# A graph attention and expert kernel: the first graph's index with evenly cut list transfers, its column cast first, and node positions found and scattered by groups of seven tiles

## The reference

```python
edge_index = jnp.stack([src, dst])                                  # 100,000 edges, 6250 nodes
x = x + gnn(_layernorm(x), edge_index, W, a_l, a_r)                 # 4 heads of 64 features
x = x + ffn(_layernorm(x)[None], W_gat, att_src, att_dst, ..., L0_ffn_edge_index)[0]   # 131,072 edges

# gnn: for each edge (row, col)
e   = leaky_relu(h_l[row] + h_r[col], 0.2)
m   = segment_max(e, row);  ex = exp(e - m[row])
att = ex / segment_sum(ex, row)[row]
out = segment_sum(att[:, :, None] * h[col], row)
```

## Time and profile before

| what | value |
|---|---|
| median of 3 runs | 3050.68 us (3048.28 to 3055.36) |
| profiled execution | 3046.62 us, span 3044.9 us |
| POOL busy | 1871.1 us (61%) |
| DVE busy | 1847.1 us (61%) |
| PE busy | 1694.7 us (56%) |
| ACT busy | 587.0 us (19%) |

### The profile page before, as it was taken

One profiled execution on the slowest core, in us unless ns is written; L12 is line 12 of the kernel. 1 busy time (PEld: TensorE's weight loads), 2 busy tenths in 40 slices (PEclk: granted clock), 3 DMA queues, 4 the chain that ended last, 5 costly groups with the idle time before them and its releaser, 6 DMA issues. The chain is left out here.

```text
span 3044.9 us, 25674 instructions
## 1 busy us (share of the span) xinstructions
PE 1694.7 (56%) x7316; PEld 1279.9 (42%) x7316; DVE 1847.1 (61%) x3710; ACT 587.0 (19%) x1135; POOL 1871.1 (61%) x1908
## 2 busy tenths in 40 slices
PE   4511430255655552666645268889797979786300
PEld 3411110234434341444335246667676767674200
DVE  7778783879977885766656224443434334347558
ACT  4300000123322220222224111212121211110000
POOL 0000457767777777777507677777777777777470
PEclk9755765677777775878775589899999999998655
DMA  5300302557666565666455322222222222227244
GB/s 160 51 0 0 95 6 77 170 192 242 222 221 200 192 224 156 211 218 228 166 207 153 78 70 43 43 53 43 55 40 46 43 43 43 43 55 212 74 127 157
DMA packets 203488, 354.57 MB, mean 116 GB/s; under 512 B 56043, under 2 KB 161442, under 8 KB 193842
## 3 DMA queue, kind: packets, MB, share of 16 engines
q0 software_dynamic: 73264, 122.14, 17.7%
q1 hardware_dynamic: 80889, 181.57, 17.0%
q10 hardware_dynamic: 49260, 50.05, 5.0%
HBM read 181.47 MB, written 171.59 MB: 116 GB/s over the span
## 5 line engine op out<-in xcount | busy, mean ns | idle before, releaser
L567 POOL DMA_INDIRECT at_ring<-table,e_col x872 | 831.9, 954 | 265.7 <-issue 265.7
L1800 POOL DMA_INDIRECT at_ring<-table,at_idx x792 | 784.4, 990 | 253.2 <-issue 233.4
L1892 PE MATMUL at_psS<-at_ring,at_hot 128*128 128x260 f32 x1584 | 436.7, 439 | 147.8 <-DVEq L1997 140.5
L1892 PEld LDWEIGHTS at_psS<-at_ring,at_hot 128*128 128x128 f32 x1584 | 319.5, 218 | 257.5 <-issue 84.3
L1368 PE MATMUL ffn_psY<-late_space 128*128 128x256 f32 x1568 | 356.9, 389 | 99.0 <-DVE late_space L1420 99.0
L1357 PE MATMUL ffn_psH<-xnT,late_space 128*128 x896 | 359.4, 561 | 69.0 <-ACT late_space L1392 60.8
L1420 DVE TENSOR_TENSOR late_space<-ffn_psY,ffn_b 128x256 f32<-128x256 f32 x196 | 82.5, 424 | 517.4 <-PE ffn_psY L1368 517.2
L1368 PEld LDWEIGHTS ffn_psY<-late_space 128*128 128x128 f32 x1568 | 305.8, 196 | 149.1 <-DVE late_space L1420 101.8
L1914 ACT ACTIVATE at_ring<-at_psS 128x520 f32<-128x520 f32 (+1 forms) x432 | 237.7, 567 | 507.7 <-PE at_psS L1892 507.7
L1357 PEld LDWEIGHTS ffn_psH<-xnT,late_space 128*128 128x128 f32 x896 | 275.4, 310 | 143.2 <-ACT late_space L1392 65.0
L1992 DVE TENSOR_TENSOR at_ring<-at_ring,at_psW 128x1024 f32<-128x1024 f32 (+1 forms) x216 | 231.5, 1127 | 27.8 <-ACT at_ring L1905 19.6
(11 more groups left out here) (367 smaller groups left out, 2169.1 us busy)
## 6 DMA issues: line engine op xcount, KB each, us to landing
at_sums<-at_ring SPq DMA_DIRECT2D x72, 1452.0 KB, 6.0
products<-late_space ACTq DMA_DIRECT2D x28, 896.0 KB
late_space<-products SPq DMA_DIRECT2D x16, 896.0 KB, 11.8
at_ring<-table,e_col POOLq DMA_INDIRECT x872
at_ring<-table,at_idx POOLq DMA_INDIRECT x792, 3.3
at_sums<-at_ring SPq DMA_DIRECT2D x16, 768.0 KB, 3.3
late_space<-products ACTq DMA_DIRECT2D x12, 896.0 KB, 11.9
table<-np_rows SPq DMA_DIRECT2D x7, 910.0 KB, 4.2
```

Source lines behind the costliest of these rows:

```text
L567: g.indirect_dma_start(self.ring[z][:, k, 0:TW], None, self.table, bass.IndirectOffsetOnAxis(ap=self.runs.col[:, u * U + k:u * U + k + 1], ...
L1800: g.indirect_dma_start(self.ring[z][:, k, 0:self.TW], None, self.table, bass.IndirectOffsetOnAxis(ap=self.idx[:, z, k:k + 1], axis=0)).the ...
L1892: last = pe.matmul(self.psS[at % 2][:, k - lo, 0:TW], self.hot[:, b, k, :], rows[:, b * self.SUB + k, 0:TW], start=True, stop=True)
```

## The change

- The list of `prior` is loaded in two transfers (112 and 15 rows), `by_chain` in two (96 and 3), and so is the second graph's shifted list in `Runs.load_prior` (112 and 15).
- DVE casts the columns to `x.col` before it waits for `even` and `prior`.
- The first graph's positions are found by groups of seven tiles, between the tiles' counts. Their PE results lie in another PSUM tile (`att.psE`), since `turned` is still in use then. POOL makes its three `row0` gathers first and waits per group of seven scatters.
- In round 0, `weigh_rows` stands ahead of `short_levels`.
- For the second graph, `positions` is the same work in three calls, with two instructions in another order.

```diff
+EVENLY = (0, 112), (112, 127)
@@ Ranks
+    def count_past(self, pe):
         for i in range(t.T):
             last = pe.matmul(self.ps_many[:, i:i + 1], t.past[:, i, :], t.one[:, :], start=True, stop=True)
         last.then_inc(self.s_many, 1)
+    def nexts(self, pe, part, lo, hi):
+        pe.wait_ge(self.s_first, part + 1)
+        pe.matmul(self.ps_next[:, lo:hi], t.shift[:, :], t.first[:, lo:hi], start=True, stop=False)
+        pe.matmul(self.ps_next[:, lo:hi], t.corner[:, :], t.first[:, lo + 1:hi + 1], start=False, stop=True)\
+            .then_inc(self.s_next, 1)
+    def bases(self, v):
+        v.wait_ge(self.s_many, 1)
+        q.step(v.tensor_scalar(t.before_t[:, :], self.ps_many, 1.0, float(self.J), ALU.subtract, ALU.mult))
+    def firsts(self, v, lo, hi):
+        v.wait_ge(self.s_used, 2 * hi + 2)
...
+        v.sem_inc(self.s_first, 1)
+    def positions(self, v, part, lo, hi, start_idx):
+        v.wait_ge(self.s_next, part + 1)
...
@@ Runs.load_prior
-        a.dma_start(self.prior[1:P, :].bitcast(F32), self.code[0:P - 1, :]).then_inc(self.s_prior, 16)
+        for lo, hi in EVENLY:
+            a.dma_start(self.prior[lo + 1:hi + 1, :].bitcast(F32), self.code[lo:hi, :]).then_inc(self.s_prior, 16)
@@ ChainRuns.load
-        sp.dma_start(self.prior[1:P, :], codes[0:P - 1, :]).then_inc(self.s_even, 16)
-        sp.dma_start(self.by_chain, self.flat[0:x.slots].rearrange("(p m) -> p m", p=CHAINS)).then_inc(self.s_chain, 16)
+        for lo, hi in EVENLY:
+            sp.dma_start(self.prior[lo + 1:hi + 1, :], codes[lo:hi, :]).then_inc(self.s_even, 16)
+        chains = self.flat[0:x.slots].rearrange("(p m) -> p m", p=CHAINS)
+        for lo, hi in (0, 96), (96, CHAINS):
+            sp.dma_start(self.by_chain[lo:hi, :], chains[lo:hi, :]).then_inc(self.s_chain, 16)
@@ ChainRuns.set_starts
+        for b in range(x.T // BATCH):
+            g.wait_ge(self.s_starts, b + 1)
+            for t in range(b * BATCH, (b + 1) * BATCH):
...
@@ ChainRuns.vector
         for t in range(x.T):
             ranks.below(v, 0, 0, t)
-        ranks.positions(v, x.start_idx[:, :])
-        v.sem_inc(self.s_starts, 1)
+            b, k = divmod(t, BATCH)
+            if t == BATCH:
+                ranks.bases(v)
+            if b and k == 0:
+                ranks.firsts(v, found, t + 1)
+                found = t + 1
+            elif b and k == 2:
+                starts(b - 1)
+        ranks.firsts(v, found, x.T)
+        starts(batches - 1)
@@ ChainRuns.tensor
             ranks.rows(pe, 0, 0, t)
-        ranks.end_rows(pe)
+            b, k = divmod(t, BATCH)
+            if t == 0:
+                ranks.count_past(pe)
+            elif b and k == 1:
+                ranks.nexts(pe, b - 1, (b - 1) * BATCH, b * BATCH)
+        ranks.nexts(pe, batches - 1, (batches - 1) * BATCH, self.index.T)
@@ block two, DVE, round 0
                         att.scores(v, n0, z)
+                        att.weigh_rows(v, n0, z)
                         order2.short_levels(v, levels)
-                        att.weigh_rows(v, n0, z)
```

More of the change, by code:

```diff
@@ L384, in below @@
                             accum_out=t.n[:, bass.ds(at + i, 1), half]).then_inc(self.s_used, 1)
[L386 to L389, removed]
+    def count_past(self, pe):
+        t = self.t
+        for i in range(t.T):
             last = pe.matmul(self.ps_many[:, i:i + 1], t.past[:, i, :], t.one[:, :], start=True, stop=True)
         last.then_inc(self.s_many, 1)
[L392 to L394 removed]
@@ L396, in positions @@
-    def positions(self, v, start_idx):
-        t, T, q = self.t, self.t.T, self.q
-        q.eng = v
[L401 to L406, removed]
-        v.wait_ge(self.s_many, 1)
-        do(v.tensor_scalar(t.before_t[:, :], self.ps_many, 1.0, float(self.J), ALU.subtract, ALU.mult))
-        do(v.tensor_tensor(t.many[:, :], t.many[:, :], t.before_t[:, :], ALU.add))
-        do(v.tensor_scalar(t.first[:, 0:T], t.many[:, :], 0.0, None, ALU.max))
-        v.sem_inc(self.s_first, 1)
[L412 to L417, removed]
+    def nexts(self, pe, part, lo, hi):
+        t = self.t
+        pe.wait_ge(self.s_first, part + 1)
+        pe.matmul(self.ps_next[:, lo:hi], t.shift[:, :], t.first[:, lo:hi], start=True, stop=False)
+        pe.matmul(self.ps_next[:, lo:hi], t.corner[:, :], t.first[:, lo + 1:hi + 1], start=False, stop=True)\
+            .then_inc(self.s_next, 1)
@@ new lines, in positions @@
+    def positions(self, v, part, lo, hi, start_idx):
+        t, q, at = self.t, self.q, slice(lo, hi)
+        q.eng = v
+        v.wait_ge(self.s_next, part + 1)
+        q.step(v.tensor_tensor(t.count[:, at], self.ps_next[:, at], t.first[:, at], ALU.subtract))
+        q.step(v.tensor_scalar(t.last[:, at], self.ps_next[:, at], 1.0, 0.0, ALU.subtract, ALU.max))
+        q.wait()
+        q.step(v.tensor_scalar(t.none[:, at], t.count[:, at], 0.0, float(NOWHERE), ALU.is_equal, ALU.mult))
+        q.wait()
+        q.step(v.tensor_tensor(t.spare_t[:, at], t.first[:, at], t.none[:, at], ALU.add))
+        q.wait()
+        q.step(v.tensor_copy(start_idx[:, at], t.spare_t[:, at]))
+        q.wait()
@@ L469, in positions @@
         x, t, q = self.index, self.ranks.t, self.q
-        self.ranks.positions(v, x.start_idx[:, :])
+        self.ranks.bases(v)
+        self.ranks.firsts(v, 0, t.T)
+        self.ranks.positions(v, 0, 0, t.T, x.start_idx)
         q.step(v.tensor_tensor(t.last[:, :], t.last[:, :], t.none[:, :], ALU.add))
@@ L1610, in set_starts @@
         x = self.index
[L1611 to L1615, removed]
         for n in range(GROUPS):
@@ L1619, in set_starts @@
                                  bounds_check=x.T * P - 1, oob_is_err=False).then_inc(self.s_row0, 16)
+        for b in range(x.T // BATCH):
+            g.wait_ge(self.s_starts, b + 1)
+            for t in range(b * BATCH, (b + 1) * BATCH):
+                g.indirect_dma_start(self.starts, bass.IndirectOffsetOnAxis(ap=x.start_idx[:, t:t + 1], axis=0),
+                                     self.own[:, t, :], None, bounds_check=x.slots - 1, oob_is_err=False)\
+                    .then_inc(self.s_set, 16)
     def vector(self, v):
@@ L1653, in vector, with starts @@
         v.sem_inc(self.s_col, 1)
+        v.wait_ge(self.s_even, 48)
+        v.wait_ge(self.att.s_iota, 1)
+        ranks.past(v, self.even)
         ranks.differences(v, self.even, self.prior, self.itmp, self.itmp2)
+        def starts(b):
+            ranks.positions(v, b, b * BATCH, (b + 1) * BATCH, x.start_idx)
+            v.sem_inc(self.s_starts, 1)
+        batches, found = x.T // BATCH, 0
         for t in range(x.T):
             ranks.below(v, 0, 0, t)
-        ranks.positions(v, x.start_idx[:, :])
-        v.sem_inc(self.s_starts, 1)
+            b, k = divmod(t, BATCH)
[8 more added lines that the diff above has]
+        starts(batches - 1)
         rowf, new = self.rowf, self.colf
```

31 lines of the change are left out of this document (23 added, 8 removed).

## The result

The changed kernel takes 2979.2 us (median of 4 runs, 2975.94 to 2986.15); the kernel before, with one more run, 3051.73. The ratio is 0.9763, 95% interval 0.9751 to 0.9776: 2.4% faster, 72.5 us. The profiled execution took 2975.94 us, span 2974.2, which is 70.7 us under the span before. Block two starts 0.9 us earlier than before and block three 70.2 us earlier (DVE's first instruction there is at 1501.93 for 1572.10), so that 69.2 us of it arise in block two.

A forecast was written before the change was run, and what follows sets the result against it. Block two was bound first by hand-overs, then POOL until about unit 14, then DVE. Savings of 40.3 + 7.2 + 26 = 73.5 us from 3046.62 gave 2973.1 profiled, median 2977; range 2962 to 3006, own bounds 2968 to 2994.

The forecast's parts named there:

- Lists and cast: Block two's start: list lands before 321.9, POOL gets its index 15.2 us earlier, DVE's first count comes 7.8 us earlier.
- Groups on DVE: First graph's positions: seven sets at 1.6 us, 11.2 in all; positions end at 412.9, 2.2 us later than before.
- groups at full price: Rival: each group's PE trip stands open (4.6 us), index 20.5 us later; 53 us off, 2998; chance 0.10.
- Scatters: POOL, block two: scatters start after row0 gathers at 371.0, keep 73.9 us without starving, done at 444.9 for 485.25.
- the slower rival: Rival: scatters beside DVE's counts take 5.12 us each, POOL ends at 622; 104 us slower, 3155; chance 0.03.
- The wait that ends last: Before the seeds' load: SP waits for DVE's index at 448.3 instead of the scatters; 2.5 us of 40 lost.
- Unit 2: POOL in block two: waits for the stored seeds until 501.7, so this unit starts 40.3 us earlier.
- Slots: Round 0: POOL's waits of 1.58 and 5.64 us for slots go, 7.2 us gained, between 0 and 7.2.
- Second list: Second graph's shifted list, late in block two: landing 10.8 us after issue, DVE's wait some 3, 26 us gained.
- signs of being wrong: POOL waiting between groups, scatters over 2 us, second-list wait over 10 us, or DVE waiting for gathers in the last rounds.
- The second list did come sooner: Rival denied here: busy DMA engines bring the second graph's list no sooner in effect; 47.5 us off, 3003; chance 0.11.
- the cut into even pieces matters: Rival denied here: pieces bring neither list sooner, DVE starts 6.7 us later than forecast; 40.8 off, 3010; chance 0.04.

The follow-up runs named there:

- a5: The changed kernel with the shifted lists' two pieces of 113 and 14 rows instead of 112 and 15: 3004.4 us, ratio 0.9854 to the kernel before.
- a2: The changed kernel with all 49 tiles' positions found at once after the counts, no groups; repeated on another chip: 3008.8 us, ratio 0.9861 to the kernel before.
- a4: The changed kernel with groups of seven kept, but POOL scattering only after the last group; repeated on another chip: 3019.9 us, ratio 0.9903 to the kernel before.
- b3: The kernel before with only the groups of seven, scatters group by group and the row0 gathers first: 3023.7 us, ratio 0.9919.
- a3: The changed kernel with short_levels ahead of weigh_rows in round 0 again; repeated on another chip: 2984.2 us, ratio 0.9786 to the kernel before.
- b1: The kernel before with only the second graph's shifted list in pieces of 112 and 15 rows: 3022.0 us, ratio 0.9907.
- c1: The changed kernel with three groups (14, 21, 14 tiles) for seven and the row0 gathers last: 2979.8 us, ratio 0.9766 to the kernel before.

## Why the prediction was right

It said 2977 us, 73.5 us off; 2979.2 and 72.5 were measured. The mechanism of block two's first 200 us was right; the 26 us of the second list came out right by luck. Point by point:

- *Lists and cast.* This was right. Both lists land early, DVE begins `past` at 322.3, the first count comes at 335.13 (forecast 335.9), and POOL's index copy at 322.3 (323.4). a5 shows the cause.
- *Groups on DVE.* The positions were forecast 2.2 us later than before; they came 1.1 later, or 2.0 counted from the block's start. DVE's wait behind the small matmuls is 1.33 us, where 2 were forecast. PE's trips are covered except the last (0.76 us). The rival of groups at full price is out: six further sets and the matmuls together cost 9.0 us (a2 against a4), and at 4.6 us a set they would have cost 28.
- *Scatters.* Their end was forecast at 444.9 and measured at 441.3. They start at 369.27, not at 371. They keep 0.98 us beside the counts and slow down, to 4.11 at most, only beside DVE's wide instructions, as before, and POOL shows no more than its usual 0.30 us between groups. The starved scatters of the slower rival would have needed 3.0 us each, pause included, only to lose what the rest gained. With the rule of the Trainium skill, "SBUF — State Buffer", section "SBUF: two separate sides", by which DVE's two-port instructions keep GpSimd from writing descriptors, the trace agrees as far as the counts go: beside them a scatter takes its usual 0.98 us.
- *The wait that ends last.* This was right: the index took the place of the scatters, and the seeds start at 447.22 (forecast 448.3). a2 and b3 show the other order, where the scatters end last.
- *Unit 2.* Its start was forecast at 501.7 and measured at 501.50. Counted from the block's start it is 0.7 later than forecast.
- *Slots.* 7.2 us were forecast, and 6.2 measured at unit 6; a3 gives 6.3 us of waits back. It also held that DVE's three new waits for exponentials (2.06 us each) cost nothing.
- *POOL after that.* The forecast carried POOL's lead to the end unchanged; 2.2 us were lost over units 6 to 23. The page has the 792 gathers at 788.3 us of busy time for 784.4. Which of DVE's instructions slow them was not tried.
- *Second list.* The term was 26 us and 26.3 arrived, but by two errors that cancel, and that is luck. The step "landing 10.8 us like the store, a wait of 3" failed: the list landed in 4 to 5 us and no wait was left, so that 28.8 us were to be had. And the step "35.1 - 3.2 = 31.9 us before it meets POOL again" failed as well: it set the distance at unit 23 against the shortest distance at unit 9. DVE is nearest to POOL at unit 21. There it starts at 1442.98, 31.8 us behind the end of the gather (POOL's next copy, 1411.18), and the shortest distance in these rounds is 5.5 us (b1). That leaves 26.3 us of room, just what came. One of the signs of being wrong that the prediction names did appear: in the changed kernel DVE waits 6.26 us at unit 21 (1372.56), for 4.42 before, so POOL did take the bound back there.
- *Rivals.* The second list did come sooner (b1), and the cut into even pieces matters (a5).
- *The range.* The forecast's own bounds, added up again from the numbers beside them, give 2971 to 2994 and not 2968 to 2994. The prediction also takes 485.25 for the end of the last scatter, which is at 484.95, and leaves out a third wait for a slot before, of 0.42 us. Nothing above hangs on these.

## What to carry to other kernels

Cut a transfer whose rows have no large divisor up to 16 so that each piece has one: one row more or less was worth 25 to 28 us here. Where one engine finds indices and another uses them, hand them over in groups small enough that the second never starves, and then look which of the two sets the next step, since in c1 the coarser cut only moved the wait; a finer one was not tried. Room before the next bound has to be read at the place where the two engines come nearest, not at the end.

## What the hardware showed beyond that

The one-engine list also held back what was queued behind it. SP's issue of `by_chain` lasted 8.44 us before, and the two issues of it take 0.93 us now. The second array of the second graph's edges (`e_val`, 512 KB) landed 16.1 us after its issue before and 8.5 us now.

```profile
307.92 8.44 SPq L1585 DMA_DIRECT2D at_ring<-e_flat  x1
```

```profile
307.60 0.93 SPq L1617 DMA_DIRECT2D at_ring<-e_flat  x2
```

The change also cut `by_chain` itself, but in a5, where `by_chain` is cut and the list's 113 rows lie on one engine, both come back: the two issues of the shifted list last 6.77 us and `e_val` lands after 17.3 us.

```profile
307.45 6.77 SPq L1614 DMA_DIRECT2D at_hot<-e_flat  x2
```
